# A four-layer conditional transformer on one core: small products issued in pieces, and the second sequence's first products moved ahead of the first attention

## The reference, cut to what matters

```python
mod = silu(c) @ w_adaln + b_adaln                      # 6 vectors of 288: shift, scale, gate, twice
h = ln(x) * (1 + sc_msa) + sh_msa
q, k, v = split(h @ w_qkv + b_qkv)                     # 16 heads of 18
o = softmax(q @ k.T * 18 ** -0.5) @ v
x = x + g_msa * (o @ w_proj + b_proj)
xn = ln(x) * (1 + sc_mlp) + sh_mlp
# layer 0: cw from the two largest of xn @ w_gate (4 logits per token); sum over 4 experts
x = x + g_mlp * sum_e cw[e] * (gelu(xn @ w1[e] + b1[e]) @ w2[e] + b2[e])
# layers 1 to 3: the same with a single expert and cw = 1
```

## Time and profile before

| what | value |
|---|---|
| time, median of 3 runs | 2198.0 us (2194.46 to 2200.98) |
| profiled execution: its own time / span | 2202.24 us / 2200.5 us |
| PE busy | 2004.8 us, 91% |
| DVE / ACT busy | 1336.7 us, 61% / 1142.4 us, 52% |
| mean granted clock of PE | 0.946 of full |
| chain that ended last | PE 61%, DVE 20%, ACT 11%, DMA 3% |

### The profile page before, as it was taken

The page is one execution under the profiler, slowest core; times in us unless marked ns, Lnnn a source line. Parts: engine busy times, 40 slices in busy tenths (PEclk is TensorE's granted clock), DMA queues, the critical chain, the costliest instruction groups (busy, mean ns, idle before and its releaser), DMA issues.

```text
span 2200.5 us, 38987 instructions
## 1 busy us (share of the span) xinstructions
PE 2004.8 (91%) x15592; PEld 1496.7 (68%) x15592; DVE 1336.7 (61%) x2940; ACT 1142.4 (52%) x1705; POOL 208.3 (9%) x311
## 2 busy tenths in 40 slices
PE   6988999899998999999899999989997898999998
PEld 4346578748974896698575566887886646474658
DVE  4747647656674677476658482463545858684842
ACT  2353734474656365545636556554344474747463
POOL 3000111111110110011110000001100000000001
PEclk9686999899989999999999999998899999999999
DMA  5234242343234232524331412446154141314101
GB/s 160 60 120 85 74 122 63 73 122 92 77 68 136 64 86 48 152 67 100 78 104 18 131 7 65 68 78 134 30 107 111 31 114 36 96 20 112 26 3 25
DMA packets 204731, 173.97 MB, mean 79 GB/s; under 512 B 54822, under 2 KB 164678, under 8 KB 204550
## 3 DMA queue, kind: packets, MB, share of 16 engines
q1 hardware_dynamic: 197974, 158.76, 31.0%
q0 software_dynamic: 6576, 12.71, 2.1%
HBM read 125.57 MB, written 40.11 MB: 75 GB/s over the span
## 4 chain that ended last, share of the span: by engine, by line
PE 61%; DVE 20%; ACT 11%; DMA 3%; issue 3%; SPq 2%; POOL 0%; ACTq 0%; POOLq 0%; DVEq 0%
PE PSA L1890 16%; PE PSA L1905 14%; DVE MX L1529 9%; PE PSA L1680 5%; PE PSA L1794 4%; PE PSA L1771 4%; PE PSA L1741 4%; ACT PB L1378 4%; PE PSA L1784 3%; PE PSA L1753 2%; DVE HH L1659 1%; PE PSA L1814 1%; PE PSA L1703 1%; DVE FL L1429 1%; ACT FH L1408 1%
## 5 line engine op out<-in xcount | busy, mean ns | idle before, releaser
L1529 DVE TENSOR_REDUCE MX<-PSA 128x1 f32<-128x512 f32 x768 | 490.2, 682 | 292.9 <-PE PSA L1771 289.8
L1890 PE MATMUL PSA<-A,FH 128*128 128x256 f32 x2520 | 442.1, 290 | 14.0 <-DVE HH L1659 9.9
L1905 PE MATMUL PSA<-FH,HH 128*128 128x288 f32 x2016 | 443.2, 311 | 3.9 <-DVE HH L1659 3.3
L1415 ACT ACTIVATE HH<-PSA 128x512 fp32r<-128x512 f32 x252 | 150.6, 598 | 561.5 <-PE PSA L1890 552.0
L1378 ACT ACTIVATE PB<-PSA 128x1024 f32<-128x1024 f32 x384 | 370.8, 1026 | 86.4 <-PE PSA L1784 85.8
L1890 PEld LDWEIGHTS PSA<-A,FH 128*128 128x128 f32 x2520 | 362.3, 194 | 37.4 <-issue 18.7
L1905 PEld LDWEIGHTS PSA<-FH,HH 128*128 128x128 f32 x2016 | 327.1, 193 | 41.0 <-issue 32.6
L1905 PE MATMUL PSA<-FL,HH 128*128 128x288 f32 x1008 | 301.7, 299 | 0.0
L1771 PE MATMUL PSA<-KS,QS 54*128 54x512 f32 x768 | 221.4, 504 | 29.8 <-DVE MX L1529 12.2
L1283 POOL TENSOR_TENSOR X<-X,TM 128x288 f32<-128x288 f32 x128 | 101.3, 809 | 1455.2 <-DVE TM L1594 1455.2
L1659 DVE TENSOR_TENSOR HH<-PSA,HH 128x512 fp32r<-128x512 f32 x252 | 172.1, 683 | 85.1 <-ACT PSA L1416 84.5
(11 more groups left out here) (171 smaller groups left out, 2258.8 us busy)
## 6 DMA issues: line engine op xcount, KB each, us to landing
qkd<-HH SPq DMA_DIRECT2D x48, 504.0 KB
ST<-in_L_cond_w SPq DMA_DIRECT2D x51, 432.0 KB
ST<-in_L_cond_w SPq DMA_DIRECT2D x102, 192.0 KB
QS<-qkd SPq DMA_DIRECT2D x88, 144.0 KB
KS<-qkd SPq DMA_DIRECT2D x88, 144.0 KB
QS<-qkd SPq DMA_DIRECT2D x144, 72.0 KB
KS<-qkd SPq DMA_DIRECT2D x144, 72.0 KB
ST<-in_L_cond_w SPq DMA_DIRECT2D x153, 48.0 KB
```

What stands on the lines that cost most here:

```text
L1415: e.activation(r(HH[u][:, 0, :]), PS[bk][:, :], gelu)
L1529: e.reduce_max(MX[p // 2 % 2][:, col:col + 1], PS[bk][:, :], axis=AX.X).then_inc(free[bk], 1)
L1890: m = e.matmul(PS[bk][:, s_ * 256:(s_ + 1) * 256], r(w_), r(x_[:, half * 256:(half + 1) * 256]), start=(z == 0), stop=(z == 6))
L1905: m = e.matmul(PS[bk][:, 0:C], r(HH[u][:, c, tk]), r(w_), start=False, stop=(j == NCH - 1 and z == 2))
```

## The change

- `ada` vectors of shift and scale are issued as three parts of 3 matmuls (`ada_col`), and the gate vectors as before; each part yields "pause", at which `step_bg` gives up its turn unless forced.
- `rt` is issued as four quarters of 7 matmuls, and `route` follows the turn without the two empty yields.
- The second sequence is loaded, its statistics, norm and turn are made at the start, as are the first three of its five qk tiles (with the values of unit 0 between); the other two come in attention 0. `at_end` now includes unit 1: its three `qkin` groups come after all five tiles.
- Unit 0's first `rows` comes right after the eighth s1 step; `LEAD` is 4, not 6, and is counted after it.
- The conditioning load (0, 1) comes before the value weights and both from SP (`SP_JOBS` 4). In unit 0's `mid` the s1 stream has a gap of 1000 ns of estimated PE time.

```diff
@@ -25,19 +25,19 @@
 NSC = 3 * NHT
 
 PE_NS = {"fc1": 1650, "fc2": 400, "proj": 930, "v": 930, "v2": 930, "qk": 1650, "turnx": 500, "turno": 500,
-         "s1": 230, "s2": 450, "av": 230, "no": 500, "rows": 350, "qk2": 1650, "s1b": 1700, "s2b": 3000, "av2": 2500, "no2": 500, "rt": 3100}
+         "s1": 230, "s2": 450, "av": 230, "no": 500, "rows": 350, "qk2": 1650, "s1b": 1700, "s2b": 3000, "av2": 2500, "no2": 500, "rt": 775}
 MID_NS = (3500, 800, 600)
-S1_0_NS = (0, 2500, 4000)
+S1_0_NS = (1000, 2500, 4000)
 S1_NS = (5000, 400, 3000)
 MID_AT = (6000, 11000)
 QK_LAND = 12000
 STK_LAND = 16000
 ST_LAND = 14000
-SP_JOBS = 3
+SP_JOBS = 4
 BG = 3
 HELD = 3
 TURN_AT = 2
-LEAD = 6
+LEAD = 4
 W_MID = 4
 DEFER = 1
 LAG = 2
@@ -135,7 +135,7 @@
         now = ring_of[0]
         return tuple(now[(ring_n[0] + 1 + k) % len(now)] for k in range(len(now)))
 
-    jobs = [("ada", 0, 0), ("q", 0), ("v", 0), ("ada", 0, 1), ("ada", 0, 2), ("wg",), ("p", 0)]
+    jobs = [("ada", 0, 0), ("q", 0), ("ada", 0, 1), ("v", 0), ("ada", 0, 2), ("wg",), ("p", 0)]
     jobs += [("f", k) for k in range(3)]
     k_ = 3
     for i_ in range(NI + 1):
@@ -241,12 +241,30 @@
             k = stage(("ada", L, j))
             for u in range(2):
                 bk = ring()
-                put("ada", L, j, u, k, landed[k], bk)
                 if 2 * j + u in (2, 5):
+                    put("ada", L, j, u, k, landed[k], bk)
                     gr_ready[L, (2 * j + u) // 3] = bk
-                else:
-                    mf_ready[L, (2 * j + u) // 3] = bk
-                yield
+                    yield "pause"
+                    continue
+                parts = [0, 1, 2]
+
+                def part():
+                    put("ada_col", L, j, u, k, landed[k], bk, parts.pop(0))
+                    if not parts:
+                        put("ada", L, j, u, k, landed[k], bk)
+                        rest.pop(bk[0], None)
+
+                def all_parts():
+                    while parts:
+                        part()
+
+                part()
+                later(bk[0], all_parts)
+                mf_ready[L, (2 * j + u) // 3] = bk
+                yield "pause"
+                while parts:
+                    part()
+                    yield "pause"
             left[k] = ("full", bk)
             ahead()
             yield
@@ -332,7 +350,7 @@
         qk_at[i, grp] = pe[0]
         put("qkin", i, p0, p1, grp, outs, s2_done[3 if i == 12 else p1 // 2 - 1])
 
-    at_end = (0,)
+    at_end = (0, 1)
 
     def proj_qk2(i):
         for t in range(5):
@@ -377,12 +395,13 @@
                 qk_in(i, 2, 4, 1, outs[3])
         if i == 12:
             return
-        if i:
-            while s2_at[0] < (i - 1, 3):
-                yield
-        else:
-            qk_in(i, 0, 2, 0, outs[1])
-            qk_in(i, 2, 4, 1, outs[3])
+        for g in range(2):
+            if i in at_end:
+                while i and s2_at[0] < (i - 1, g):
+                    yield
+                qk_in(i, 2 * g, 2 * g + 2, g, outs[2 * g + 1])
+        while i and s2_at[0] < (i - 1, 3):
+            yield
         qk_in(i, 4, 8, 2, outs[4])
         qkd_free[i % 2] = tuple(qk_n)
         yield
@@ -447,6 +466,10 @@
                     yield
             if p % 2:
                 late = (g, bk)
+            if i == 0 and p == 1:
+                rows(*late)
+                late = None
+                yield
         yield
         rows(*late)
         yield
@@ -610,8 +633,23 @@
 
     def route(i):
         bk = ring()
-        put("rt", i, bk, a_ready[(i + 1) % 2], w_ready["wg",])
+        qs = [0, 1, 2, 3]
+
+        def quarter():
+            put("rt", i, bk, a_ready[(i + 1) % 2], w_ready["wg",], qs.pop(0))
+            if not qs:
+                rest.pop(bk[0], None)
+
+        def all_quarters():
+            while qs:
+                quarter()
+
+        quarter()
+        later(bk[0], all_quarters)
         yield
+        while qs:
+            quarter()
+            yield
         put("rt0", i)
         for j in range(4):
             put("rtk", i, j)
@@ -627,8 +665,11 @@
 
     def step_bg(n):
         while n > 0 and bg:
-            if next(bg[0], "end") == "end":
+            got = next(bg[0], "end")
+            if got == "end":
                 bg.pop(0)
+            elif got == "pause" and not forced[0]:
+                return
             else:
                 n -= 1
 
@@ -785,19 +824,28 @@
     put("x", 0)
     ahead()
     ahead()
+    put("x", 1)
     drain(stats(0, 1))
     ada0 = ada(0)
-    for _ in range(3):
-        next(ada0)
+    while next(ada0) == "pause":
+        pass
     drain(split(("q", 0), "q"))
     normed(0, 1, n_norm[0])
     drain(turn_x(norm_of[0], 0, 0, 0, 0))
+    drain(stats(1, 0))
     drain(proj_qk(0))
+    normed(1, 0, n_norm[0])
+    while next(ada0) == "pause":
+        pass
     drain(split(("v", 0), "v"))
+    pre1 = pre(1)
+    for _ in range(3):
+        next(pre1)
     proj_v(0)
-    put("x", 1)
     for _ in range(3):
-        next(ada0)
+        next(pre1)
+    for k in range(8):
+        settle(k)
     put("msk")
     forced[0] = False
     bg += [ada0, split(("wg",), "wg"), split(("p", 0), "p")]
@@ -808,7 +856,7 @@
         if i < NI:
             nxt = pre(i + 1) if i + 1 < NI else iter(())
             if i == 0:
-                nxt = itertools.chain(norm(1), nxt)
+                nxt = pre1
             if i + 1 < NI and (i + 1) // 4 != 2:
                 stream.append(s1_steps(i + 1))
             ring_of[0] = RING_A2 if L == 2 else RING_A
@@ -1605,7 +1653,9 @@
                     w.wait_ge(free[bk], n + 1)
                     e.tensor_tensor(x, x, TD[:, :], ALU.add).then_inc(s_resmid, 1)
                 elif kind == "rt":
-                    i, (bk, n), _, _ = a
+                    i, (bk, n), _, _, q = a
+                    if q < QT - 1:
+                        continue
                     w.wait_ge(full[bk], n + 1)
                     e.tensor_copy(GL[:, :, :].rearrange("p q e -> p (q e)"), PS[bk][:, 0:16]).then_inc(free[bk], 1)
                     logits = (bk, n)
@@ -1686,23 +1736,31 @@
                     L, j, u, k, land, (bk, n) = a
                     v = 2 * j + u
                     s = ST[k % 2]
-                    w.wait_ge(s_sl, 2)
-                    w.wait_ge(s_stf[k % 2] if k < SP_JOBS else s_st[k % 2], land)
-                    may_fill(bk, n)
                     if v in (2, 5):
+                        w.wait_ge(s_sl, 2)
+                        w.wait_ge(s_stf[k % 2] if k < SP_JOBS else s_st[k % 2], land)
+                        may_fill(bk, n)
                         for c in range(3):
                             kk = 128 if c < 2 else 33
                             m = e.matmul(PS[bk][0:4, 0:C], SL[0:kk, c, :],
                                          s[0:kk, c * 2 * C + u * C:c * 2 * C + u * C + C],
                                          start=(c == 0), stop=(c == 2))
-                    else:
-                        for c, np_ in ((0, 128), (1, 128), (2, 32)):
-                            for x in range(3):
-                                kk = 128 if x < 2 else 33
-                                base = x * 2 * C + u * C + c * 128
-                                m = e.matmul(PS[bk][0:np_, 4 * c:4 * c + 4], s[0:kk, base:base + np_],
-                                             SL[0:kk, x, :], start=(x == 0), stop=(x == 2))
-                    m.then_inc(full[bk], 1)
+                        m.then_inc(full[bk], 1)
+                elif kind == "ada_col":
+                    L, j, u, k, land, (bk, n), c = a
+                    s = ST[k % 2]
+                    w.wait_ge(s_sl, 2)
+                    w.wait_ge(s_stf[k % 2] if k < SP_JOBS else s_st[k % 2], land)
+                    if c == 0:
+                        may_fill(bk, n)
+                    np_ = 128 if c < 2 else 32
+                    for x in range(3):
+                        kk = 128 if x < 2 else 33
+                        base = x * 2 * C + u * C + c * 128
+                        m = e.matmul(PS[bk][0:np_, 4 * c:4 * c + 4], s[0:kk, base:base + np_],
+                                     SL[0:kk, x, :], start=(x == 0), stop=(x == 2))
+                    if c == 2:
+                        m.then_inc(full[bk], 1)
                 elif kind in ("turnx", "turnx2"):
                     c, slot, m, (bk, n), *_, ot = a
                     rows = OT if ot else XN
@@ -1863,17 +1921,18 @@
                     token_rows(A[(i + 1) % 2], [WP[:, 0, :], WP[:, 1, :]], [WPL[:, 0, :], WPL[:, 1, :]],
                                WP[:, 2, :], q, bk).then_inc(full[bk], 1)
                 elif kind == "rt":
-                    i, (bk, n), ready, wm = a
+                    i, (bk, n), ready, wm, q = a
                     tt = terms(A[(i + 1) % 2], [WG[:, 0, :], WG[:, 1, :]], [WGL[:, 0, :], WGL[:, 1, :]], WG[:, 2, :], rows=96)
                     a_wait(ready)
```

(13 more changed lines are left out.)

## The result

| | before | after |
|---|---|---|
| median of 4 runs each | 2198.6 us (2194.5 to 2201.0) | 2219.1 us (2213.4 to 2226.9) |
| ratio, 95% interval | | 1.010 (1.007 to 1.013) |
| span of the profiled execution | 2200.5 us | 2218.2 us |

The kernel is 1% slower, where 1.6% faster was forecast. The page of the kernel after: busy time of PE, and the granted clock in 40 slices.

The account below looks back on a forecast made before the run. PE was taken to bound the kernel after 197 us, a chain through DVE before. Shift -20 after attention 1, -17 for the clock, +1.5 for weights: -35.5 from 2202.2, or 2163 us on the median's scale, range 2142 to 2185.

Parts of the forecast that it names:

- term 2: Attention 0: added qk tiles and 12 more s1 steps mostly hidden, +0.5 us, bounds -8 and +8.
- term 5: Moved maxima and gate product work cost +4 us in the feed-forward of unit 0 and +4 in attention 1.
- Term 1: Start up to the first score step: unit 1's early work against fewer maxima, +2.5 us.
- Rival C: Attention 0: the clock rises earlier, five more iterations at full clock, -9 us or so, 2153; chance 0.08.
- Terms 3 and 4: 132 to 197 us: unit 1's tiles and 32 maxima leave; running shift -5.5 us at first projection, -28 at first `fc1`.
- Term 6: Gate and conditioning products elsewhere: pieces among dense work keep the clock up, -17 us, bounds 0 and -24.
- Rival A: Small products: the pieces don't hold the clock and its dips stay, 2180 us; chance 0.15.
- my sign of being wrong in 6: Windows around gate and conditioning products keeping clocks near 0.8 would refute the -17 us clock gain.
- Term 7: Feed-forward with conditioning pieces, layer 0: next expert's weights come later, one more wait, +1.5 us.
- Rival D: Attention 0: thin pieces keep the clock at half throughout, +30 us or more there, 2209.5; chance 0.05.

Follow-up runs that it names:

- e12: The kernel before with only the first row maxima sent at once and `LEAD` 4 instead of 6: 2220.7 us, ratio to before 1.0080.
- e3: The change with `LEAD` 8 instead of 4: 2199.1 us, ratio to before 1.0018.
- e5: e3 with gate and conditioning products whole again, no pieces: 2192.4 us, ratio to before 0.9972.
- e7: e3 with only the gate products whole again, conditioning still in pieces: 2193.6 us, ratio to before 0.9980.
- e9: The change with `LEAD` 6 instead of 4: 2202.8 us, ratio to before 1.0021.
- e6: e5 with the s1 gap in the feed-forward of unit 0 at 1500 instead of 2500 ns: 2190.6 us, ratio to before 0.9940.
- e11: e6 with the first row maxima sent two s1 steps later and `LEAD` 6: 2191.2 us, ratio to before 0.9968.
- e2: The kernel before with only the pieces and the background's pause added: 2199.5 us, ratio to before 1.0004.
- e4: The change with two s1 steps per score step in attention 1 as well: 2211.2 us, ratio to before 1.0069.
- e8: e5 with two s1 steps per score step in attention 1 as well: 2194.1 us, ratio to before 0.9971.
- e10: e6 with the conditioning products in pieces again, gate products whole: 2196.1 us, ratio to before 0.9986.

## Why the prediction was wrong

Between the forecast for the profiled execution, 2166.7, and the 2219.9 us that it took lie 53.2 us: 15.0 in term 2, 12.8 in the attention 1 of term 5, 23.2 in terms 6 and 7 together, and 2.2 in all the rest.

**Term 1, first score step +2.5:** measured +1.3, and s1 began at 50.9 us, not 53. Right. But its remark that `rows` "now leaves only 8 maxima (4.9 us) to land behind" priced the fewer steps for the first rows only.

**Term 2, attention 0 at +0.5, is one step that failed: it was +15.5.** I counted the DVE time of 12 more s1 steps and found it hidden, which the busy times bear out (45.0 of 80 us). What I did not count is lead: steps taken from ahead of a stage are taken from the distance between every later `rows` and its reader. The way from a group's last maximum to its reader took 5.4 and 7.5 us in the trace, against iterations of 3.2 us at full clock: it needs more than one iteration's distance, and the change left none. e12 makes the loss alone (+0.8%), e3 takes it away. Rival C came true beside it, the clock rising some 16 us earlier, and was more than lost in the waits and in the falls of the clock that began in them.

**Terms 3 and 4 held:** -8.2 for the 8.5 of term 3, and -19.7 for 22.5; 25.4 us from projection to `fc1`, forecast 23. **Term 5** had the feed-forward right (+4.3 for 4). That its gain is no gain, the quarters' work only moving from the one stage to the other, e5 and e7 show. **Its attention 1, +4, was +16.8**: the same failure, with a queue on top, which held the rows up by 1.1 us here and by 4.9 in e9. I had priced maxima by DVE's time, and not looked at what stood on SP ahead of `rows`. e6 and e11, with the same early unit 1 and the rows back in place, need 49.6 and 49.1 us there.

**Term 6, -17, was 0** (e2: 1.0004), and terms 6 and 7 together +7.7 in the profiled execution and not -15.5. Its mean clock was 0.949, not 0.96 to 0.97. Of the 7.7 us only 3.6 lie ahead of unit 2's first score step, where the weights came late; four kernels with the same pieces needed 1923.7 (the change), 1919.8 (e9), 1918.5 (e2) and 1912.5 us (e4) behind attention 1, one profile each, and the kernel before 1915.9, so that the rest can't be told from what differs between executions. Rival A, the pieces don't hold the clock, was right in its sum. The changed kernel's windows at the places of the earlier trace rows show how:

```profile
425.00:437.00 12.00, 11.73 (x89) 10.60 (x88) 7.42 (x15) 5.16 (x9) 3.66 (x6) 1.00 0.00 0
617.00:629.00 12.00, 12.00 (x96) 11.44 (x94) 8.80 (x18) 5.82 (x11) 1.56 (x2) 1.00 0.56 159
828.00:840.00 12.00, 12.00 (x96) 11.42 (x94) 8.82 (x18) 5.82 (x11) 1.56 (x2) 1.00 0.57 161
1135.00:1165.00 30.00, 27.91 (x193) 22.22 (x191) 19.76 (x43) 6.77 (x13) 3.33 (x6) 1.00 0.16 48
1530.00:1560.00 30.00, 28.66 (x237) 27.14 (x239) 9.30 (x21) 7.25 (x14) 1.74 (x3) 0.66 0.45 85
```

Four of the five are up and the last is lower, so my sign of being wrong in 6, that "windows like the earlier trace rows keep clocks near 0.8", stayed away in four. The sum was wrong because it took a fall that goes for time gained. Behind attention 1 the half clock went from 134.5 to 127.3 us only; falls came back at the starts of attentions and around the conditioning of layer 3, and from unit 2's first score step to unit 3's it is 13.7 us at half clock and 213 us in both kernels. The Trainium skill's rule in rival A ("TensorE: Matmul & The Clock Gate", Part 1), that the clock falls when PE idles, gives the right sum; that the falls at the gate products went while PE was as busy as before is not told by it.

**Term 7, +1.5:** PE waits for weights in the feed-forward of unit 0 (294 to 445 us) after:

```profile
PE PSA L1949 <- DVE FL L1477: 5.4, 4, 2.7
PE PSA L1949 <- ACT FH L1456: 5.1, 4, 2.0
```

10.5 us where before 6.8 stood in that stretch (4.7 for the fix, 2.1 for the split): +3.7, of the forecast kind and over twice its size. Over the whole kernel these waits went from 10.9 to 16.0 us, those for the fix alone, which the earlier trace rows counts, from 7.5 to 9.6.

**Rival D**, the slower one, had the right sign and the wrong mechanism: the clock was not held down from the start, it fell behind waits for DMAs that no case of mine held. The old trace held that wait in six places, one of them in attention 1 (1.0 us), and I had not taken it up:

```profile
PE PSA L1784 <- DMA QS<-M: 8.5, 6, 3.6
```

## What to carry to other kernels

- Work that runs ahead in a stream is not only load, it is distance. Before steps are taken from the front of such a stream, list for each product of it where it is issued and where it is read, before and after, and price the whole way (last input, what stands ahead on the engine that copies it, issues on the queue and what stands ahead of them there, landing) against what lies between.
- A fall of the clock that goes at one place is worth nothing until the sum over all that follows has fallen too. Take the half-clock time of the whole rest as the measure, not a window.
- Where a change of many parts loses, its parts can be right: here the same early start with eight steps of lead, whole products and the maxima in their old places is 0.6% faster than before.

## What the runs showed of the hardware

- Half clock in attention 0 varies without any wait for rows: 17.0 us in e3 and e8, 18.2 in e6, 23.9 in e5, 28.6 in e11, 42.7 in e7, 48.9 in e10, and the stage lasts 66.6 to 78.9 us with it. In e7 and e10 a fall of 17.1 us began behind PE pauses of 0.4 to 1.1 us each, most of them for maxima. One profile each doesn't tell whether kernel or execution decides that; it stays open, and with it what part of the differences of up to 5.5 us between e5, e6, e7, e10 and e11 is theirs.
- Three falls in the attentions of the changed kernel lasted 13.7 us each. Two began 2.3 and 2.0 us into waits of 4.5 and 3.8 us, the third 1.5 us ahead of a wait of 6.0.
- The landing of the four small `QS<-M` DMAs took 1.76 us three times and 3.11 us once, with 0.62 to 0.98 us for each issue on SP: in the 4.36 us ahead of the score product at 109.89 the issues on the chain take 2.0 us, a little more than the landing.
